# Second pass of a Mamba block: state 0's output is written by ScalarE, and the skip term is added by accumulating DMAs

## The reference

```python
def step(h, inp):                    # h: [batch, 1024 channels, 16 states]
    dA_t, dBu_t, C_t = inp
    h = dA_t * h + dBu_t             # dA = exp(dt * A), dBu = dt * B * u
    y_t = jnp.einsum('bdn,bn->bd', h, C_t)
    return (h, y_t)
...
y = ys.swapaxes(0, 1) + u * Dskip    # the skip term
y = y * jax.nn.silu(z)
return y @ W_out.T
```

## Time and profile before

| | |
|---|---|
| median of three runs | 2877.29 us (2876.44 to 2885.26) |
| profiled execution | 2876.51 us, span from first to last instruction 2874.4 us |
| PE busy | 2412.2 us, 84% of the span |
| DVE busy | 2379.2 us, 83% |
| ACT busy | 2044.6 us, 71% |
| POOL busy | 1845.6 us, 64% |
| second pass | from about 1088 us, 16 chunks, about 107 us each |
| mean granted TensorE clock | 0.921 |

### The profile page before, as it was taken

How to read it: one execution, slowest core, us unless ns; L and a number is a source line. 1 busy time by engine, 2 the same in 40 slices (tenths; PEclk the granted TensorE clock), 3 DMA queues, 4 the chain that set the end, 5 groups by cost and what they waited for, 6 DMA issues and landing times.

```text
span 2874.4 us, 37734 instructions
## 1 busy us (share of the span) xinstructions
PE 2412.2 (84%) x12448; PEld 1386.4 (48%) x12448; DVE 2379.2 (83%) x3197; ACT 2044.6 (71%) x3775; POOL 1845.6 (64%) x1449
## 2 busy tenths in 40 slices
PE   3577998998998843698998998998998998998988
PEld 1233444444443313555555555555555555555554
DVE  6556667667667556999999999999999999999992
ACT  2233667667657675788888888888888888888883
POOL 1112223222222117999999999999999999999991
PEclk8788999999999866799999999999999999999999
DMA  6553333333232337657767767766767767767744
GB/s 206 176 205 139 126 107 114 115 114 122 100 133 87 112 107 247 159 131 169 169 151 169 168 155 167 171 149 169 170 148 167 170 148 170 168 147 171 171 104 101
DMA packets 200289, 429.25 MB, mean 149 GB/s; under 512 B 44512, under 2 KB 93920, under 8 KB 199840
## 3 DMA queue, kind: packets, MB, share of 16 engines
q1 hardware_dynamic: 160928, 284.23, 29.8%
q0 software_dynamic: 39168, 142.62, 26.7%
HBM read 190.86 MB, written 110.10 MB: 105 GB/s over the span
## 4 chain that ended last, share of the span: by engine, by line
POOL 33%; DVE 14%; PE 8%; issue 7%; ACT 0%; DMA 0%; POOLq 0%; SPq 0%; DVEq 0%; ACTq 0%
POOL dbu L1075 25%; DVE h L1294 9%; POOL y L1094 4%; PE p_g L1432 3%; DVE y L1307 3%; PE p_ht L1398 2%; POOL y L1109 1%; PE p_g L1441 1%; POOL dbu L1080 1%; PE p_g L1422 1%; POOL x L1113 1%; DVE x L1341 0%; POOL carry L1086 0%; DVE x L1331 0%; POOL small L70 0%
## 5 line engine op out<-in xcount | busy, mean ns | idle before, releaser
L1075 POOL TENSOR_TENSOR dbu<-dtu,bb 128x1024 f32<-128x1024 f32 x512 | 1268.3, 2612 | 20.3 <-DVE h L1294 20.0
L1294 DVE TENSOR_TENSOR_SCAN h<-p_da,dbu 128x512 f32<-128x512 f32 x1024 | 1187.3, 1207 | 34.7 <-POOL dbu L1080 18.1
L1168 ACT ACTIVATE p_da<-dt,neg_a 128x255 f32<-128x255 f32 x2048 | 879.6, 467 | 243.6 <-DVE h L1294 237.9
L1398 PE MATMUL p_ht<-ident,h 128*128 128x128 f32 x4096 | 564.3, 297 | 131.5 <-DVE h L1294 130.8
L1398 PEld LDWEIGHTS p_ht<-ident,h 128*128 128x128 f32 x4096 | 513.6, 154 | 208.2 <-DVE h L1294 183.3
L1307 DVE SCALAR_TENSOR_TENSOR y<-p_ht,ct,y 128x1024 f32<-128x1024 f32 x272 | 345.1, 1269 | 19.3 <-PE p_ht L1398 19.0
L714 PE MATMUL p_u<-xz,wu 128*128 128x512 f16 x1536 | 350.0, 385 | 6.8 <-DVE xz L508 6.2
L1432 PE MATMUL p_g<-wo,tokt 128*128 128x512 f16 x1536 | 352.3, 387 | 2.9 <-ACT tokt L1211 1.6
L1441 PE MATMUL p_g<-wz,xz 128*128 128x512 f16 x1536 | 344.5, 381 | 0.0
L70 POOL TENSOR_TENSOR small<-small,consts 128x1 f32<-128x1 f32 x96 | 68.8, 717 | 423.4 <-DVE small L63 423.4
L363 POOL TENSOR_TENSOR late<-dt,u 128x512 f32<-128x512 f32 x64 | 81.6, 1274 | 376.5 <-DVE dt L561 376.5
(11 more groups left out here) (118 smaller groups left out, 2805.4 us busy)
## 6 DMA issues: line engine op xcount, KB each, us to landing
y<-y_part POOLq DMA_DIRECT2D x224, 512.0 KB, 5.7
bb<-b_scratch SPq DMA_DIRECT2D x128, 256.0 KB, 4.0
xin<-in_x SPq DMA_DIRECT2D x32, 512.0 KB, 5.4
x_scratch<-x SPq DMA_DIRECT2D x32, 512.0 KB, 5.2
xz_scratch<-xz SPq DMA_DIRECT2D x16, 1024.0 KB, 6.2
y_scratch<-late SPq DMA_DIRECT2D x32, 512.0 KB, 5.4
dt_scratch<-dt SPq DMA_DIRECT2D x64, 256.0 KB, 2.1
dtu_scratch<-late SPq DMA_DIRECT2D x64, 256.0 KB, 2.4
```

What stands on the lines that cost most here:

```text
L1075: nc.gpsimd.tensor_tensor(state[:, 4 * f:4 * f + 4, :], dtu[k % 3][:], bb[n // NB % 2][:, n % NB:n % NB + 1, :].to_broadcast([P, G // 2, T2]),
L1168: ins_ = nc.scalar.activation(p_da[p % 2][:, k * T2 + 1:(k + 1) * T2], dt[m % NR][:, k, 1:], ACT.Exp, scale=neg_a[:, g, n:n + 1])
L1294: nc.vector.tensor_tensor_scan(h[n % 2][:, 2 * p:2 * p + 2, :].rearrange("p g t -> p (g t)"), p_da[p % 2][:], dbu[n % 2][:, 2 * p:2 * p + ...
L1398: mm = nc.tensor.transpose(p_ht[t][:, g * P:(g + 1) * P], h[n % 2][:, g, t * P:(t + 1) * P], ident[:])
```

## The change

The skip term no longer stands in y when state 0 comes. ACT writes C * h of state 0 into both y tiles (first_state), with no reading of y: t = 0 in slot 1 ahead of the low halves and of decays 2 and 3, t = 1 behind them. POOL then issues an accumulating DMA from y0 in DRAM into each tile (add_y0): t = 0 between the two halves of the products of state 2, t = 1 behind them. SP's load_y is gone. DVE begins with state 1; that one addition stands behind all four scans of slot 2 and waits for y0 of t = 0, the other 14 stay between the halves. The first part that is summed into y[par][1] waits for y0 of t = 1. The core of the diff:

```diff
@@ sync
-                def load_y(c, par):
-                    if not (isinstance(c, int) and c < 2):
-                        b, m = place(c - 1, "t", 1, 1)
-                        wait_alone(sp, g_full[b], m + 1)
-                    for t in range(TT2):
-                        sp.dma_start(y[par][t][:], dram["y0"][bass.ds(c * T2 + t * P, P), :]).then_inc(y_loaded[par], 16)
...
-                        if z_on and more(i) and n == 9:
-                            load_y(i + 1, 1 - par)
@@ gpsimd
                     for f in range(2):
+                        if n == 2 and f:
+                            add_y0(i, par, 0)
...
+                def add_y0(c, par, t):
+                    wait(pool, y_added[t], c * NS + 1)
+                    pool.dma_start(y[par][t][:], dram["y0"][bass.ds(c * T2 + t * P, P), :],
+                                   accum_op=ALU.add).then_inc(y0_added[par][t], 16)
...
                     if sums.index(n):
                         wait(pool, *summed(c, sums[sums.index(n) - 1]))
+                    elif n in Y_SUM:
+                        wait(pool, y0_added[cpar][1], (c // 2 + 1) * 16)
...
                             times_b(i, par, n)
+                            if n == 2:
+                                add_y0(i, par, 1)
@@ scalar
+                def first_state(i, par, t):
+                    if t == 0:
+                        wait(act, ct_loaded[par], (i - par) * 8 + 16)
+                        if i >= 2:
+                            b, m = place(i - 1, "t", 1, 1)
+                            wait(act, g_full[b], m + 1)
+                    wait(act, ht_full[t], i * NS + 1)
+                    nc.scalar.activation(y[par][t][:], p_ht[t][:], ACT.Copy, scale=ct[par][:, t, 0:1]
+                                         ).then_inc(y_added[t], 1)
...
+                        if z_on and n == 1:
+                            first_state(i, par, 0)
                         for unit in halves_before(i, n):
                             low(*unit)
...
                             decays(i, par, n, (2, 3))
+                            if n == 1:
+                                first_state(i, par, 1)
@@ vector
-                    if n == 0:
-                        wait(dve, y_loaded[par], (c - par) * 16 + 32)
+                    if n == 1:
+                        wait(dve, y0_added[par][t], (c // 2 + 1) * 16)
                         wait(dve, ct_loaded[par], (c - par) * 8 + 16)
...
-                        add_state_before(i, par, n, 0)
+                        if n != 2:
+                            add_state_before(i, par, n)
...
                         if z_on:
                             scans(i, n, 1)
-                        add_state_before(i, par, n, 1)
+                        if n == 2:
+                            add_state_before(i, par, n)
```

More of the change, by code:

```diff
@@ L836, in second_pass @@
         y_summed, y2_summed = [sem(f"y{i}_part_summed") for i in range(2)], sem("y2_part_summed")
-        y_loaded = [sem(f"y2_loaded{i}") for i in range(2)]
+        y0_added = [[sem(f"y0_added{i}{t}") for t in range(TT2)] for i in range(2)]
         b_loaded = [sem(f"b2_loaded{i}") for i in range(2)]
@@ L1004, in prologue @@
                     load_edge(1)
-                    load_y(0, 0)
                     load_xz(0)
@@ L1178, in part_state @@
                 def part_state(i, par, n):
-                    if n == PARTED[0]:
-                        wait(act, ct_loaded[par], (i - par) * 8 + 16)
                     if n == Y2_FIRST:
@@ L1298, in add_state @@
                 def add_state(c, par, n, t):
-                    if t and n in PARTED:
-                        return
-                    if n == 0:
-                        wait(dve, y_loaded[par], (c - par) * 16 + 32)
+                    if n == 1:
+                        wait(dve, y0_added[par][t], (c // 2 + 1) * 16)
                         wait(dve, ct_loaded[par], (c - par) * 8 + 16)
-                    else:
-                        wait(dve, y_added[t], c * NS + n)
+                    wait(dve, y_added[t], c * NS + n)
                     wait(dve, ht_full[t], c * NS + n + 1)
@@ L1308, in add_state, with add_state_before @@
                                                    in1=y[par][t][:], op0=ALU.mult, op1=ALU.add).then_inc(y_added[t], 1)
-                def add_state_before(i, par, n, t):
-                    if n and flags(i)[2]:
-                        add_state(i, par, n - 1, t)
+                def add_state_before(i, par, n):
+                    if n >= 2 and flags(i)[2]:
+                        add_state(i, par, n - 1, 0)
                     if n == 0 and flags(i)[1]:
-                        add_state(i - 1, 1 - par, NS - 1, t)
+                        add_state(i - 1, 1 - par, NS - 1, 0)
                 def silu_part(i, t, x):
```

## The result

| | before | changed |
|---|---|---|
| median (lowest to highest, runs) | 2877.23 us (2876.44 to 2885.26, 4 runs) | 2917.82 us (2916.54 to 2918.99, 4 runs) |
| ratio, with its 95% interval | | 1.0135 [1.0116, 1.0153] |
| profiled execution, span | 2874.4 us | 2917.2 us |

The changed kernel is 40.6 us slower; 2916 was forecast. Measured again later, the same kernel took 2916.98 us against 2882.38, ratio 1.0116 [1.0097, 1.0136]. Other names for lines: the scans are L1307 now, DVE's additions L1317, the products of POOL L1067, the carry L1072, the new transfers of y0 L1076, ACT's copies of state 0 L1200, the transposes L1410.

The account below looks back on a forecast made before the run. DVE was taken as the bound nearly everywhere, POOL at state 3 as second, 1.5 us behind. Losses of 2.9 us in six chunks, 2.2 in ten, together 39.4 on 2876.5, gave 2916 us; range 2886 to 2950.

Parts of the forecast that it names:

- The mechanism: At each chunk's turn, state 0's scan sets ACT's copy, the copy sets POOL, POOL sets DVE's state 3; 109.8 us a chunk.
- The wait itself: POOL idles for ACT's copy between the halves of state 2's products, 2.1 to 2.9 us in 14 chunks or more.
- a sign of being wrong: The prediction called itself wrong if POOL's wait for ACT's copy in mid state 2 was under 1 us.
- The turn, term by term: Mid state 2 to state 3: second half 3.5 or 2.8 us late, second issue 0.9, less 1.5: 2.9 or 2.2.
- The 1.5 us of idle and lead: POOL's idle before the merge plus its lead over DVE at state 3, 1.5 to 1.6 us, absorbs part of the delay.
- The issue: Each new DMA issue at the turn holds POOL 0.61 to 0.88 us, against the skill page's 50 ns dispatch.
- DVE is the bound nearly everywhere: In the second pass DVE sets the pace; POOL at state 3 of each chunk is a second bound, 1.5 us behind.
- DVE's saving goes into waits for decays: The 2.36 us a chunk DVE saves at state 0 becomes waits for decays at state 1, 1.6 to 2.7 us.
- The transfer of y0: The accumulating DMA into y lands in 7.3 us before DVE needs it; costs 0, at most 3 us a chunk.
- No change: Rival: ACT's copy is there when POOL asks, only the issues cost, 0 to 0.5 us a chunk; 2877 to 2885; chance 9%.
- A part of it: Rival: some of DVE's waits fall away or issues are cheaper, 1 to 1.6 us a chunk; 2893 to 2902; chance 16%.
- The faster case: Rival: DVE is the bound at state 3 too, up to 38 us gained, 2839 us; chance 6%.

Follow-up runs that it names:

- the last run: The kernel before without DVE's two additions of state 0, a one-column memset for each, no copies or transfers for them, state 0's output missing: 2873.22 us, ratio 0.9963.

## Why the prediction held, point by point

- **The mechanism** held: POOL's wait in the middle of state 2 sets state 3 of DVE, once a chunk. All fourteen starts of state 3 from chunk 2 to 15 have a wait for dbu of 2.56 to 3.12 us (forecast 2 to 3), POOL stands for ACT's copy in all fourteen turns, the merge's wait is gone, and a chunk takes 109.65 us (forecast 109.8).
- **The wait itself was over-sized**, and the delay behind it under-sized. 2.1 to 2.9 us of idle in 14 chunks or more were forecast, 2.5 in the mean; it came in every turn, but with 0.92 to 3.33 us, 2.0 in the mean, 1.15 in the turn shown. Two of the fourteen (0.92 and 0.95) are under the 1 us that the prediction had named as a sign of being wrong; the shift at state 3 is there in both (2.57 us). The forecast took POOL's place against PE from the trace of before, where its first half ended with PE's start (2063.92 against 2063.87). In the changed kernel it ends at 1979.83, 1.47 us behind PE's start at 1978.36, and 1.0 in the mean: POOL now leaves each turn with no lead on DVE (0.04 us instead of 0.5 in the mean) and makes none on the way, as its waits for DVE's scans have gone from 16.8 us to 2.5. What counts for the end is not the idle but when the second half starts against PE's transposes.
- **The turn, term by term**, in a turn with PE at full clock: the second half starts 3.23 us behind the start of PE's transposes, where it was 0.05, so 3.2 later (forecast 2.8: the copy came 0.1 us later than forecast and the issue 0.3 behind it). From the end of the second half to that of the gate it is 3.71 us (1984.26 to 1987.97), before 2.74 (2066.57 to 2069.31): 0.97 for the second issue (forecast 0.88). The 1.5 us of idle and lead are gone (forecast 1.5). 3.2 + 1.0 - 1.5 = 2.7 at state 3 (forecast 2.2 in such a turn). Over chunks 2 to 15, from the start of the transposes of state 0 to state 3 of DVE it is 16.1 us in the mean, before 13.1: 2.9 more (forecast 2.5). From there to the next state 0 it is 93.6, before 94.1: 0.5 less, where the forecast said that nothing gets shorter. 2.9 - 0.5 = 2.4 remain. That the total was met within 2 us is luck in part: two errors of 0.4 to 0.5 us a chunk, 7 to 8 us each in the total, went against each other.
- **The issue.** By the Trainium skill, page "DMA: Bandwidth & Descriptors", section "Anatomy of one DMA — SWDGE (gpsimd) path", the dispatch takes some 50 ns and generation is small. The runs speak against that here: two issues of 4 KB that nothing waits for lengthen POOL's turn by 0.93 and 0.97 us and the kernel by 9.4 us.
- **The bound was read one-sidedly.** "DVE is the bound nearly everywhere" rested on waits: 1.3 us for POOL, 34.7 for others. The chain that ended last in the page of before says "POOL 33%; DVE 14%". Neither alone is right: with 0.9 us a chunk less on POOL nothing is gained, and with 2.36 less on DVE 0.3 to 0.7 a chunk. In a near tie the chain's shares tell little: in the kernel before with one issue less, which takes the same time, they are DVE 35% and POOL 4%; in the changed kernel DVE 30% and POOL 10%.
- **DVE's saving goes into waits for decays**: held. 1.89 us at state 1 of the turn shown (forecast 1.6 to 2.7), 25.1 us more in all. But it wasn't needed for the loss, as the saving brought 0.7 us a chunk at most even without copies.
- **The transfer of y0** was priced at nothing, with a landing of 7.3 us. It landed in 6.4 in the median, and no wait for it is in the changed kernel. The merge landed in 5.7 us instead of 4.5, and part 15 waited for it in one turn (0.5 us). The 3 us that were kept as the other end are not seen here; with both issues back to back 0.9 of them came.
- **The rivals.** "No change" would have needed ACT's copy ahead of POOL. "A part of it" (2893 to 2902) did not come; even with both copies first it is 2904. The faster case asked for a reserve of POOL of 6.1 us; it had 1.5, and DVE's own room was 0.5.
- **Busy times**: DVE -34.9 us (forecast -40), ACT +32.8 (+35), POOL +31.0; 32 issues of 0.89 make 28.5 of it.

What stays open: why the first pass's length differs by up to 5 us between profiles, which makes single spans uncertain by 0.2%; why the rest of a chunk, from state 3 on, is 0.5 us shorter; and whether any other place for the copies, outside slot 1, would keep the 10 us of the last run. No version with a complete result beat the kernel before.

## What to carry to other kernels

When work is moved off a nearly full engine, first take it away altogether, in the profile or on the chip: if that gains little, no place for it will gain more. A wait in front of one piece of an engine's in-order queue is paid by all that stands behind it, and putting it elsewhere only pays if what it waits for is also made earlier, without pushing back something else that is due. Idle time ahead of a transfer's landing is slack for added work, not a reserve for going faster: what a faster engine can gain is only the time for which its input already lies ready.

## What the runs showed of the hardware

- A DMA issue of POOL between two of its tensor operations costs 0.93 to 0.97 us of POOL, of which the engine shows 0.61 from the issue to the next start; the rest is in what follows: the gate's two instructions take 2.80 us behind an issue and 2.50 without. It is the same for 4 KB and for 512 KB.
- An accumulating DMA of 512 KB from DRAM into y lands in 6.4 us in the median (6.8 with two back to back, 7.9 where it is issued in slot 3), the one of the bias into x1 in 7.1 to 7.3, and the merge of SBUF into SBUF in 4.5 us alone, 5.7 in the changed kernel, where the second of these is issued 3.1 us ahead of it, and 7.4 where both are issued within 3.6 us ahead of it.
